# Cross attention of a decoder layer: a convolution kernel's products in four column groups, turned back through SBUF

## The reference, cut to what matters

```python
# softmax(q k^T) v over the 6404 context rows, first layer (all four heads as one of width 128)
# second layer, S4D: its convolution kernel K, needed later
dt = exp(log_dt);  dtA = dt[:, None] * (A_re + 1j * A_im)         # 128 channels d, 64 states n
dC = C * (exp(dtA) - 1) / (A_re + 1j * A_im)
K  = 2 * einsum('dn,dnl->dl', dC, exp(dtA[:, :, None] * arange(1024))).real
```

## Time and profile before

| | |
|---|---|
| time before, median of 3 runs | 1744.25 us (1743.5 to 1744.35) |
| the profiled execution's own time | 1739.54 us |
| its span, first to last instruction | 1737.8 us |
| PE busy | 1420.6 us, 82% of the span |
| DVE, ACT, POOL busy | 74%, 54%, 40% |
| mean granted TensorE clock | 0.912 of full speed |

### The profile page before, as it was taken

One profiled execution on the slowest core, in us unless ns is written; L12 is line 12 of the kernel. 1 busy time (PEld: TensorE's weight loads), 2 busy tenths in 40 slices (PEclk: granted clock), 3 DMA queues, 4 the chain that ended last, 5 costly groups with the idle time before them and its releaser, 6 DMA issues. The chain is left out here.

```text
span 1737.8 us, 19863 instructions
## 1 busy us (share of the span) xinstructions
PE 1420.6 (82%) x6581; PEld 752.1 (43%) x6637; DVE 1288.2 (74%) x3067; ACT 930.5 (54%) x1452; POOL 697.0 (40%) x529
## 2 busy tenths in 40 slices
PE   5777899899986747889898888988859339999798
PEld 2233344345544421355454554545547223333365
DVE  4998677855427539999999999999857666777433
ACT  4665212556521310788888888888831225666321
POOL 0664312012000000698898988989930030000012
PEclk9899899999987867999999999999888758999999
DMA  6000110000009320000000000000011030000000
GB/s 145 1 1 0 39 61 29 0 1 0 0 19 198 68 64 1 1 1 1 1 1 1 1 1 1 1 1 1 1 27 71 22 80 1 1 1 1 1 1 12
DMA packets 30968, 37.36 MB, mean 21 GB/s; under 512 B 13889, under 2 KB 24096, under 8 KB 29732
## 3 DMA queue, kind: packets, MB, share of 16 engines
q1 hardware_dynamic: 29312, 24.19, 5.1%
q10 hardware_dynamic: 1544, 11.79, 3.3%
HBM read 29.73 MB, written 6.24 MB: 21 GB/s over the span
## 5 line engine op out<-in xcount | busy, mean ns | idle before, releaser
L1461 PE MATMUL psum<-film_ka,film_context_qa 97*128 97x512 bf16 (+1 forms) x832 | 326.0, 393 | 86.8 <-DVE search_and_weigh_e L1695 36.5
L1665 DVE MAX8 search_and_weigh_kept<-psum 128x8 f32<-128x171 f32 (+2 forms) x1216 | 330.1, 324 | 0.2
L1463 PE MATMUL psum<-film_kb,film_context_qb 128*128 128x512 bf16 (+1 forms) x777 | 302.0, 390 | 0.0
L1847 ACT ACTIVATE search_and_weigh_e<-psum,search_and_weigh_bias 128x512 f32<-128x512 f32 (+1 forms) x416 | 267.5, 665 | 58.0 <-PE psum L1463 54.7
L1695 DVE SCALAR_TENSOR_TENSOR search_and_weigh_e<-psum,film_context_top,search_and_weigh_e 128x512 f32<-128x512 f32 (+1 forms) x283 | 200.0, 714 | 15.5 <-ACT search_and_weigh_e L1847 14.0
L1718 POOL TENSOR_TENSOR search_and_weigh_e<-search_and_weigh_e,search_and_weigh_keep 128x512 f32<-128x512 f32 (+1 forms) x133 | 150.6, 1132 | 108.6 <-ACT search_and_weigh_keep L1826 105.3
L1461 PEld LDWEIGHTS psum<-film_ka,film_context_qa 97*128 97x128 bf16 x832 | 86.3, 104 | 229.8 <-DVE search_and_weigh_e L1695 95.5
L1722 POOL TENSOR_TENSOR search_and_weigh_mean<-search_and_weigh_e 128x512 f32<-128x512 f32 (+1 forms) x104 | 133.4, 1283 | 11.5 <-DVE search_and_weigh_e L1695 4.4
L1752 PEld LDWEIGHTS psum<-ctx_rows,search_and_weigh_mean_T 128*128 128x128 f32 (+1 forms) x816 | 124.1, 195 | 31.3 <-issue 5.2
L2959 POOL TENSOR_TENSOR residual<-residual,top_expert_kept 128x1024 f32<-128x1024 f32 x7 | 16.5, 2355 | 292.2 <-DVE top_expert_kept L2916 292.2
L1727 POOL TENSOR_TENSOR search_and_weigh_mean<-search_and_weigh_mean,search_and_weigh_e 128x512 f32<-128x512 f32 (+1 forms) x104 | 127.9, 1230 | 8.2
(11 more groups left out here) (544 smaller groups left out, 2660.1 us busy)
## 6 DMA issues: line engine op xcount, KB each, us to landing
film_kb<-film_k_rows ACTq DMA_DIRECT2D x4, 1601.0 KB
film_ka<-film_k_rows ACTq DMA_DIRECT2D x3, 1601.0 KB
ctx_T<-in_ctx_T SPq DMA_DIRECT2D x1, 2401.5 KB
gqa_experts_w<-in_L_ffn_W SPq DMA_DIRECT2D x1, 2048.0 KB
film_convolve_back<-in_dft_back SPq DMA_DIRECT2D x1, 1728.0 KB, 11.9
film_k_rows<-cross_attention_film_hi SPq DMA_DIRECT2D x6, 256.0 KB, 2.0
film_k_rows<-cross_attention_film_mid SPq DMA_DIRECT2D x6, 256.0 KB, 2.0
film_k_rows<-cross_attention_film_low SPq DMA_DIRECT2D x6, 256.0 KB, 2.0
```

The lines of the kernel that those rows point to most:

```text
L1461: pe.matmul(out, a["qa"][0:ROWS, h, rows], a["ka"][0:ROWS, h, c + b:c + b + cols], start=True, stop=False)
L1463: last = pe.matmul(out, a["qb"][:, h, rows], a["kb"][:, h, c + b:c + b + cols], start=False, stop=True)
L1665: last = dve.max(kept[:, h % 2, first + s, :], bank[:, lo:hi])
L1847: act.activation(e[:, n % RING, sub, 0:PIECES[u][1]], ps[:, SEARCH_BANKS + q % WEIGH_BANKS, 0:PIECES[u][1]], ACT.Exp, bias=bias[:, i % 2, ...
```

## The change

The 8 products of a group now have `left` as the stationary operand (8 columns) and the powers moving (128 columns). The eight results of a group are 8 rows by 128, and they go to four column groups of PE: channel c of the group to PSUM partitions 32 (c mod 4) to 32 (c mod 4) + 7 of bank 4. Two groups (PER_BANK = 16 channels) fill the 512 columns of that one bank; this is a round r, and there are 8 of them.

As i now lies along the free axis, each round is turned back: ACT copies the whole bank to an SBUF tile `rows` (128x512), PE transposes it in four 128x128 pieces into bank 5, and ACT copies the wanted 128 columns of bank 5 into `k_tok`. Bank 4 is set to zero once by DVE, at the head of its S4D work, since the products write only 32 of its 128 partitions.

The places in the lists: ACT's copy of round r stands ahead of the sine step and of the exponential at k = 20 + 4r (20, 24, ..., 48); PE's transposes of round r ahead of the scores at k = 21 + 4r, behind that block's products where it has some; ACT's copy into `k_tok` ahead of the exponential at k = 22 + 4r. New waits: from group 2 on, PE's products of each even group wait for ACT's copy of the round before them; the transposes wait for ACT's copy of their round, and for the former `k_tok` copy. DVE's wait for a free ring slot is now on the products' own semaphore `k_rows`. The old copy of two banks behind the loop is gone.

```diff
-def s4d_vector(dve, link, k):
+def s4d_vector(dve, link, k, bank):
     sem = k["sem"]
+    dve.memset(bank, 0.0).then_inc(sem["zeroed"], 1)
...
         if q >= RING_Q:
-            dve.wait_ge(sem["k_psum"], q - RING_Q + 1)
+            dve.wait_ge(sem["k_rows"], q - RING_Q + 1)
...
-def s4d_copy(act, k, banks):
-    act.wait_ge(k["sem"]["k_psum"], NG)
-    act.activation(k["k_tok"][:], banks.rearrange("p b (d j) -> p j (b d)", j=NT),
-                   ACT.Copy).then_inc(k["sem"]["k_ready"], 1)
-
-
-def s4d_tensor(pe, k, banks, q):
+def s4d_copy_rows(act, k, bank, r):
+    sem = k["sem"]
+    act.wait_ge(sem["k_rows"], 2 * (r + 1))
+    if r >= 1:
+        act.wait_ge(sem["k_psum"], r)
+    act.activation(k["rows"][:], bank, ACT.Copy).then_inc(sem["rows_copied"], 1)
+
+
+def s4d_copy_kernel(act, k, bank, r):
+    sem = k["sem"]
+    act.wait_ge(sem["k_psum"], r + 1)
+    act.activation(k["k_tok"][:, :, r * PER_BANK:(r + 1) * PER_BANK],
+                   bank.rearrange("p (n x) -> p x n", x=32)[:, 0:NT, :], ACT.Copy).then_inc(sem["k_ready"], 1)
+
+
+def s4d_tensor(pe, k, bank, q):
     sem = k["sem"]
     if q == 0:
         pe.wait_ge(sem["left_ready"], 1)
+        pe.wait_ge(sem["zeroed"], 1)
+    if q >= 2 and q % 2 == 0:
+        pe.wait_ge(sem["rows_copied"], q // 2)
     pe.wait_ge(sem["powers"], q + 1)
     for c in range(GROUP):
         d = q * GROUP + c
-        last = pe.matmul(banks[:, d // 64, (d % 64) * NT:(d % 64 + 1) * NT], k["i_angle"][:, q % RING_Q, c, :],
-                         k["left"][:, d, :], start=True, stop=True)
+        slot = d % PER_BANK // 4
+        last = pe.matmul(bank[32 * (c % 4):32 * (c % 4) + NT, slot * P:(slot + 1) * P], k["left"][:, d, :],
+                         k["i_angle"][:, q % RING_Q, c, :], start=True, stop=True,
+                         tile_position=(0, 32 * (c % 4)))
+    last.then_inc(sem["k_rows"], 1)
+
+
+def s4d_turn(pe, k, bank, r):
+    sem = k["sem"]
+    pe.wait_ge(sem["rows_copied"], r + 1)
+    if r >= 1:
+        pe.wait_ge(sem["k_ready"], r)
+    for slot in range(4):
+        last = pe.transpose(bank[:, slot * P:(slot + 1) * P], k["rows"][:, slot * P:(slot + 1) * P],
+                            k["ident"][:])
     last.then_inc(sem["k_psum"], 1)
...
@@ PE's list
                 if k in s4d_products:
-                    s4d_tensor(pe, s4d, s4d_banks, s4d_products[k])
+                    s4d_tensor(pe, s4d, ps[:, 4, :], s4d_products[k])
+                if k - 1 in s4d_rows:
+                    s4d_turn(pe, s4d, ps[:, 5, :], s4d_rows[k - 1])
...
@@ ACT's list
+                if k in s4d_rows:
+                    s4d_copy_rows(act, s4d, ps[:, 4, :], s4d_rows[k])
                 if k in s4d_steps:
                     s4d_scalar(act, s4d, s4d_steps[k])
+                if k - 2 in s4d_rows:
+                    s4d_copy_kernel(act, s4d, ps[:, 5, :], s4d_rows[k - 2])
...
-            s4d_copy(act, s4d, s4d_banks)
```

More of the change, by code:

```diff
@@ L493 @@
 RING_Q = 4
+PER_BANK = 2 * GROUP
 def s4d_buffers(g, m):
@@ L516, in s4d_buffers @@
     k["d_skip"] = m.sb("s4d_d_skip", [1, D])
+    k["rows"] = m.sb("s4d_rows", [P, HALF])
+    k["ident"] = g["ident"]
     k["sem"] = {n: m.sem(f"s4d_{n}") for n in (
         "loaded", "dt_ready", "parts_ready", "small_ready", "small_done", "j_ready", "j_done",
-        "left_ready", "i_ready", "sin_done", "grown", "decayed", "powers", "k_psum", "k_ready")}
+        "left_ready", "i_ready", "sin_done", "grown", "decayed", "powers", "zeroed", "k_rows", "rows_copied",
+        "k_psum", "k_ready")}
     k["k_tok"] = g["k_tok"]
@@ L633, in s4d_vector @@
     power(NG - 1)
-    dve.wait_ge(sem["k_ready"], 1)
+    dve.wait_ge(sem["k_ready"], D // PER_BANK)
     link(dve.tensor_tensor(k["k_tok"][0:1, 0, :], k["k_tok"][0:1, 0, :], k["d_skip"][:], ALU.add))
@@ L706 @@
 S4D_PE_AT, S4D_PE_EVERY = 17, 2
+S4D_ROWS_AT = S4D_PE_AT + S4D_PE_EVERY + 1
 UNITS = [(c, min(CHUNK, S2 - c)) for c in range(0, S2, CHUNK)]
@@ L875, in cross_attention @@
     key_units = {KEYS_FIRST + KEYS_EVERY * u: u for u in range(len(UNITS))}
-    s4d_banks = ps[:, 4:6, :]
     s4d_steps = dict(zip(S4D_AT, range(1, S4D_STEPS)))
     s4d_products = {S4D_PE_AT + S4D_PE_EVERY * q: q for q in range(NG)}
+    s4d_rows = {S4D_ROWS_AT + 2 * S4D_PE_EVERY * r: r for r in range(D // PER_BANK)}
     def chunk_cols(c):
@@ L930, in _ @@
             dve.tensor_scalar(minus_top[:, :, DC], top[:], -1.0, None, ALU.mult).then_inc(top_ready, 1)
-            s4d_vector(dve, link, s4d)
+            s4d_vector(dve, link, s4d, ps[:, 4, :])
             dve.wait_ge(pv_done, KT)
```

## The result

The changed kernel took 1733.8 us, median of 7 runs (1728.49 to 1736.85), beside 1742.27 us for 7 runs of the kernel before. The ratio is 0.9943, 95% interval 0.9929 to 0.9957: 9.9 us faster, where 5.5 was forecast. Measured a second time beside other runs, the ratio was 0.9947 (0.9929 to 0.9964). Faster was right, the size was not, and the median lies under the forecast range. Part of that is the base: the forecast of 1738.7 us started from 1744.25 us, the median of 3 runs, and 7 runs give 1742.27. Of the 4.9 us between forecast and result 2.0 are this; the ratio is free of it.

A forecast was written before the change was run, and what follows sets the result against it. PE was taken to bound the score loop, with ACT's chain pacing behind each sine step. Terms -9.4 + 3.0 + 0.9 = -5.5 us from 1744.25 gave 1738.7 us; range 1735 to 1745.5, likeliest case 1736 to 1741.

The forecast's parts named there:

- A group of products: PE's score loop: a group costs 0.74 us instead of 1.78, saving 1.04 in each of nine groups, 9.4 us.
- The rival without overlap: Column groups do not overlap: 2.02 us a group, +6.1 us in total, 1750.3 us; chance 0.06.
- The rule of the Trainium skill: Weights load overlaps a running matmul only where row groups differ; loads and passes here would queue up to 2.02 us.
- ACT's big copy: 128x512 copy lengthens ACT's chain ahead of the sines by 0.50 us, six times: 3.0 us lost.
- The halves: Four-block pattern of the loop, split in two: half with the sine step 9.32 us, the other 8.73 - 1.04.
- The clock at the new waits: PE's seven new gaps of 1.2 us behind sine steps: clock expected to stay at 1.00.
- The rival of the falling clock: Clock falls at PE's seven new gaps, 1.8 us each, all seven 12.6: 1751.3 us; chance 0.09.
- The transposes of rounds 6 and 7: On PE, not hidden behind a wait for ACT: 2 x 0.45 = 0.9 us lost.
- the small copy: ACT's 128x128 copy behind an exponential: hidden, costing nothing; were the cover gone, 8 x 0.2 us.
- the memset: DVE's 0.49 us ahead of its chain to ACT's first sine: hidden; without that slack 0.49 us once.
- What follows the loop waits for its end and moves with it: Program behind the score loop: shifts with the loop's end, so the whole program gains the loop's 5.5 us.

The follow-up runs named there:

- the first experiment: Changed kernel with all products sent to one column group, overwriting one another in bank 4: ratio 1.0008 to the kernel before, loop 223.3 us.
- the changed kernel with one repeat: Changed kernel with PE making the scores of block 49 once more: ratio 0.9937 to the kernel before, loop 214.6 us.
- with three: Changed kernel with PE repeating the scores of block 49 three times: ratio 0.9960 to the kernel before, loop 217.2 us.
- with one repeat: Said of the kernel before: that kernel with the scores of block 49 repeated once: ratio 1.0006, loop 219.0 us.
- with two: Kernel before with the scores of block 49 repeated twice: ratio 1.0020, loop 220.7 us.

## Why the prediction was wrong

- **A group of products**, 0.74 us forecast: 0.75. Right, each part too: 16 passes in 0.56 (0.43 + 0.11 forecast), 0.09 ahead, 0.10 behind. The rival without overlap is refuted by the row, and priced by the first experiment.
- **The rule of the Trainium skill** (TensorE: Matmul & The Clock Gate, section The mechanism) that a load overlaps only where row groups differ: by the prediction's sum from it, a group costs 2.02 us. In one column group the passes take 1.84 start to start, in four 0.56, with all rows used in both. The rule does not hold back different column groups here.
- **ACT's big copy**, 0.50 forecast, 0.49 read, and 2.9 us for the six in paced halves when all eight were moved to DVE. Right.
- **The halves**, 9.32 and 7.69 forecast: 9.31 and 7.70. PE waits 1.13, forecast 1.2.
- **The clock at the new waits** (seven gaps of 1.03 to 1.13 us): no fall, as held likelier. The rival of the falling clock is gone.
- **The transposes of rounds 6 and 7, the small copy, the memset**: their sum is inside the loop's 5.5 us, which came out to a tenth; none was measured alone, so a tenth is closer than the parts are known, and partly luck.
- **What failed**: "What follows the loop waits for its end and moves with it. Against the profiled execution that gives 1739.54 - 5.5". The loop's end does move what follows. But the rest of the program was put at no change, and that step failed: PE's jump at line 1489, 770 us behind the loop, became 3.1 us cheaper in the traces, since the change put 78 more instructions ahead of it. The term was missing from the sum, and no instruction near it was edited. It is not all of the excess: in the times it is worth 1.4 to 2.8 us, and the remainder is open.

The sum by what the runs showed: 5.5 in the loop and 3.1 at the branch are 8.6 us, against 9.9 and 9.2 measured, each uncertain by 2.4 to 3. For these two that is an account within the measurement. Elsewhere it is not. For the version with DVE's copies 8.5 + 3.1 = 11.6 us stand against 16 (13.4 to 18.6); for the changed kernel with one repeat 3.1 + 3.1 against 11 (8.0 to 13.9); with three 0.4 + 3.1 against 7.0 (4.2 to 9.8). Some 4 us are left in these, outside the intervals and always to the same side, though all three share the same runs of the kernel before. Two candidates: the stretch between the loop and the branch region, 1.2 us shorter in the changed kernel's two traces, for which no cause was looked for (in the kernel before it took 773.3 us with one repeat and 776.3 with two); and the clock behind the early gaps, which in one execution gave the changed kernel's loop another 3.3 us. How often that happens in the runs whose time alone was taken is not known, and it stays open.

## What to carry to other kernels

Price an edit in its loop by rows, as here, but do not take the rest of the program as fixed when instructions are added or removed ahead of a jump: look for branch instructions behind the edit on the engine whose code length changes. Of the two in the branch region here one took either 0.4 or some 3.5 us, the other stayed between 4.6 and 5.6. To tell such an effect from a real one, look for an instruction fetch ahead of the branch in the trace, pad the kernel before with waits that are already met until the lengths agree, and compare again. And small products that use few columns of PE are worth turning round into column groups, provided that the copies this needs go to an engine that idles (DVE here) and not into the chain that sets the pace.

## What the runs showed of the hardware

- A jump of PE took 0.35 to 0.47 us or 3.3 to 3.8 us, by the place of the code alone: long at 0, 8, 16, 256 and 264, short at 51, 78, 86, 102, 128, 173 and 320 instructions. The long one ends 1.4 to 1.5 us after a 16,384-byte instruction transfer that starts within it.
- A PE gap of 2.85 us ahead of the same work was followed by the lower level of the clock in 16 of 17 traces and by the full one in one of them; 3.3 us of the loop hang on this gap and the one of 1.78 us behind it.
- Seven PE gaps of 1.03 to 1.13 us between long passes brought no fall of the clock.
- 16 passes of 128 fp32 columns took 0.56 us in four column groups and 1.84 us in one.
